# The order in which a head's query tiles have their row maxima sought, in self attention

## The chip, the cores and the metric

The kernel is one decoder layer in float32, written by hand in Bass with explicit semaphores. It runs on one core of a Trainium2 chip. The metric is the device time of one execution in microseconds (us), as the median of several executions.

## What is computed

The layer has three parts. Batch 4, sequence 1024, width 512, 16 heads of 32.

```python
x = _layernorm(tgt, n1_g, n1_b)
tgt = tgt + _block_sparse_self_attn(x, ...)     # causal, and keys/queries masked by a router
x = _layernorm(tgt, n2_g, n2_b)
tgt = tgt + _mha_cross(x, memory, ...)
x = _layernorm(tgt, n3_g, n3_b)
ff = jax.nn.relu(x @ ff_w1.T + ff_b1) @ ff_w2.T + ff_b2
return tgt + ff
```

The self attention is what the change touches:

```python
scores = jnp.einsum('bhqd,bhkd->bhqk', q, kh) / jnp.sqrt(jnp.float32(D))
...
causal = jnp.triu(jnp.ones((S, S), bool), k=1)
scores = jnp.where(causal[None, None], -jnp.inf, scores)
p = jax.nn.softmax(scores, axis=-1)
out = jnp.einsum('bhqk,bhkd->bhqd', p, vh)
```

## The kernel before

Both attentions come from one builder, `attention`; its tag is `b_` for the self attention (causal) and `e_` for the cross attention. A **group** is 4 heads of one batch entry; there are 16 groups, n = 0 to 15. While group n's softmax and output are computed, the row maxima of group n+1 are sought, because the softmax subtracts each query's maximum and the maxima have to be known before the scores proper are computed.

A **unit** is one query tile (128 queries) of one head: 8 tiles by 4 heads are 32 units. For unit u the tensor engine multiplies the tile's queries with the keys up to its diagonal (`max_scores`, L1200, tile name `b_nat`): tile t has (t+1) x 128 keys, so tile 0 has 128 and tile 7 has 1024. Up to 512 keys fill one PSUM bank, more of them two. VectorE then adds the causal mask and takes the row maximum in one custom instruction plus a short one that reads its accumulator (`maximum`, L1107) into one column of `b_neg_max`. Four PSUM banks serve this, counted 0 to 3. `bank_of` says which bank a unit begins in, and `reach` says how many units back the last user of those banks stands: with reach 2 the matmuls of unit u wait until the maximum of unit u-2 is done, with reach 3 until that of unit u-3 is.

```python
bank_of = [(0, 1, 2, 3, 0, 2, 0, 2)[u % KT] for u in range(UNITS)]
reach = [(2, 3, 3, 4, 3, 2, 2, 2)[u % KT] for u in range(UNITS)]
def unit_before(n, u):
    ...
    return n * UNITS + u + 1 - reach[u]
```

When all 32 maxima of a group are there, `turn_max` (L1206) transposes `b_neg_max` on the tensor engine into bank `TURN_BANK`; this is **the turn**. VectorE splits the result into a high and a low part (`split_max`, L1117 and L1119), and two DMAs put them as extra rows into the queries `b_qs` of the next group, for which that group's first scores wait.

The main work of a group are 12 **steps** k of 4 heads j: scores (L1217), exponential on ScalarE (L1029), additions on GpSimd (L1054), the product with the values (`weigh`, L1229, after head 2 of the next step), and twice per group a product with ones that sums the probabilities (`sum_up`, L1241; 24 records for query half 1 in step 3, 8 for half 0 in step 7). VectorE takes these sums through two transposes and a reciprocal (`invert`, L1128 to L1132) and copies the outputs out of PSUM (`copy_outs`, L1095). All engines work through their queues strictly in the order written.

Where each unit stands between the scores is set by `slot_of`: the planner gives each place (step k, head 0 or 1) some free time, and deals the units out in proportion to `unit_size`, their estimated time. Places are counted from TURN_HEAD in step 9, so that a group's maxima begin right behind the turn of the group before. In the last piece of the projection stage ahead (tile names `p_`), all 32 units of group 0 are done in eight batches of four, one batch behind each item of 12 matmuls (`leading`); the turn and the first units of group 1 (`early_units`) follow.

Of the kernel before, what the change touches and what calls it, by code (L numbers as in the profile page):

```python
# [7 lines left out]
ALU = mybir.AluOpType  # L8
ACT = mybir.ActivationFunctionType
AX = mybir.AxisListType  # L10
# [4 lines left out]
P = 128  # L15
B, S, D = 4, 1024, 512
# [11 lines left out]
KT = S // P  # L28
# [782 lines left out]
def attention(place, tag, sem, ident, q_hi, q_lo, k_hi, k_lo, v, out, vacated, keep=None, mask_qk=None,  # L811
# [6 lines left out]
    causal = keep is not None  # L818
    MAX_ROW = AUG + 1 if causal else AUG
    ROWS = MAX_ROW + 2  # L820


    steps = [(h, t, max(0, t * P - h * TOK) if causal else 0) for h in range(HALVES)
             for t in range((h + 1) * TOK // P if causal else KT)]
    last_step = {h: max(n for n, st in enumerate(steps) if st[0] == h) for h in range(HALVES)}
    NS, NBLOCKS = len(steps), len(steps) * HG
    UNITS = HG * KT
    TURN, TURN_HEAD, PE_TURN_HEAD, TURN_BANK = NS - 3, 2, 2 if causal else 3, 2

# [44 lines left out]
    for at in range(NBLOCKS):  # L876
        k, j = divmod((START + at) % NBLOCKS, HG)
        step_us = 0.3 + 3.1 * (TOK - steps[k][2]) / TOK
        free.append(max(0.1, step_us - busy[k]) / 2 if j in (0, 1) else 0)
    slot_of, acc = [], 0.0  # L880
    unit_size = [0.15 + 0.133 * ((u % KT) + 1 if causal else KT) for u in range(UNITS)]
    for u in range(UNITS):
        x, at = acc / sum(unit_size) * sum(free), 0
        while x >= free[at]:
# [13 lines left out]
        assert len(slot_of) == UNITS  # L898

    if causal:  # L900
        bank_of = [(0, 1, 2, 3, 0, 2, 0, 2)[u % KT] for u in range(UNITS)]
        reach = [(2, 3, 3, 4, 3, 2, 2, 2)[u % KT] for u in range(UNITS)]
    else:
        bank_of, reach = [u % 2 * 2 for u in range(UNITS)], [2] * UNITS

    def unit_bank(n, u):
        return 0 if narrow and n == 0 else bank_of[u]
# [20 lines left out]
    neg_max = place(tag + "neg_max", SMALL_AT + 256, [P, UNITS])  # L928
# [159 lines left out]
    def vector(dve):  # L1088
# [6 lines left out]
            dve.tensor_copy(outs[:, h, :], pv_ps).then_inc(outs_copied, 1)  # L1095

        def maximum(n, u):
            keys = ((u % KT) + 1) * P if causal else S
            banks = 2 if keys > 512 else 1
            dve.wait_ge(nat_ready, n * UNITS + u + 1)  # L1100
            if u == 0 and n >= 1:
                dve.wait_ge(max_turned, n)
            found = nat(unit_bank(n, u), banks)[:, :, 0:keys // banks]
            if causal:

                masked = mask_qk[:, S - keys:S].rearrange("p (b t) -> p b t", b=banks)
                dve.tensor_tensor_reduce(out=found, in0=found, in1=masked, scale=-1.0, scalar=3.0e38, op0=ALU.add,  # L1107
                                         op1=ALU.min, accum_out=neg_max[:, u:u + 1]).then_inc(maxed, 1)
            else:
                dve.tensor_reduce(neg_max[:, u:u + 1], found, AX.XY, ALU.max, negate=True).then_inc(maxed, 1)  # L1110

        def split_max(n):
            dve.wait_ge(max_turned, n + 1)
# [58 lines left out]
    def tensor(pe):  # L1172
# [8 lines left out]

        def max_scores(n, u):
            p = n % SETS
            j, t = divmod(u, KT)
            keys = (t + 1) * P if causal else S
            banks = 2 if keys > 512 else 1
            width = keys // banks
            rows = AUG + 1 if causal else AUG
            if u == 0:
                kept = KEPT if causal and p == 2 else 0  # L1190
                pe.wait_ge(loaded[p], ((n // SETS + 1) * LOADS + kept) * 16)
                if not causal and n < SETS:
                    pe.wait_ge(rows_set, n + 1)
            if bank_of[u] == TURN_BANK and u <= TURN_BANK and n >= 1:
                pe.wait_ge(max_split, n * 2)
            if unit_before(n, u) > 0:
                pe.wait_ge(maxed, unit_before(n, u))
            for bank in range(banks):
                cols = max(width, 256)
                last = pe.matmul(nat(unit_bank(n, u) + bank, 1)[:, 0, 0:cols], qs[p][0:rows, j, t * P:(t + 1) * P],  # L1200
                                 ks[p][0:rows, j, bank * width:bank * width + cols], start=True, stop=True)
            last.then_inc(nat_ready, 1)
# [860 lines left out]
```

## Time and profile before

| | us |
|---|---|
| median of 3 runs | 3193.87 |
| lowest and highest | 3188.46, 3200.21 |
| the profiled execution | 3189.28 |
| span of its trace | 3187.6 |

The trace covers the span from the first to the last instruction of the program, and the execution takes 1.7 us more than the span. The tensor engine (PE) is busy for most of it. In the views, PE is the matmuls, PEld the loads of their stationary operand, DVE is VectorE, ACT ScalarE, POOL GpSimd, and L followed by a number is the line of the kernel. A time in brackets is how long the engine stood idle ahead of the row, with what ended it. A tensor engine that waits for a semaphore shows as such an idle time; the matmuls behind it in its queue wait too.

### The profile page before, as it was taken

To read this page: it belongs to the slowest core of one execution; us is meant where nothing else is said; L and a number is where in the kernel's file an instruction comes from. 1 tells how busy PE (TensorE), PEld (TensorE's weight loads), DVE (VectorE), ACT (ScalarE), POOL (GpSimd) and SP (SyncE) were. 2 spreads that over 40 slices of the span, in tenths; PEclk is the share of its full clock that TensorE was granted. 3 is DMA by queue.
4 is the path that set the end of the run, shared out by engine and by line. 5 is a ranking of instruction groups with operands and counts; after the bars stand their busy time and mean duration, and the time that the engine had idled before them with its cause. 6 is when DMAs were issued, how large, how long until landed. Compare 5 with 4: busy or idle time off the path is not lost.

```text
span 3187.6 us, 39475 instructions
## 1 busy us (share of the span) xinstructions
PE 2980.7 (94%) x15242; PEld 1966.3 (62%) x15242; DVE 1758.3 (55%) x2864; ACT 1243.5 (39%) x2335; POOL 1907.5 (60%) x991
## 2 busy tenths in 40 slices
PE   7999999999999959789999999999879999999999
PEld 6888886444444427664444444444348888888887
DVE  4455656777777535666777777777742222222221
ACT  2212222555555533325666666666532111111111
POOL 3324333888888775437888888888768343333432
PEclk8999999999999979999999999999989999999999
DMA  6555774445455135734234242332122101011000
GB/s 208 176 165 186 227 220 127 107 108 111 108 117 116 41 119 184 212 133 105 63 72 89 54 104 57 79 82 58 54 67 89 40 27 40 14 40 33 34 14 14
DMA packets 199538, 310.17 MB, mean 97 GB/s; under 512 B 15011, under 2 KB 93363, under 8 KB 199347
## 3 DMA queue, kind: packets, MB, share of 16 engines
q1 hardware_dynamic: 199350, 307.64, 35.3%
q8 instruction: 121, 1.98, 0.3%
q14 instruction: 67, 0.55, 0.1%
HBM read 189.04 MB, written 117.44 MB: 96 GB/s over the span
## 4 chain that ended last, share of the span: by engine, by line
PE 53%; DVE 5%; DMA 2%; POOL 1%; issue 1%; ACT 1%; SPq 1%; DVEq 0%; POOLq 0%; ACTq 0%
PE m_ring L89 13%; PE m_o_ps L89 10%; PE e_st L1217 8%; PE e_pv L1229 7%; PE e_nat L1200 7%; PE c_ring L89 5%; PE e_st L1241 2%; DVE e_neg_max L1110 2%; DMA e_qs<-e_max_lo 1%; DMA c_x<-in_x 1%; DVE m_xt_lo L1577 1%; DMA c_w_raw<-in_ca_in_w 0%; DVE m_xt_hi L1575 0%; DVE m_ow_lo L1595 0%; DVE m_xn L1570 0%
## 5 line engine op out<-in xcount | busy, mean ns | idle before, releaser
L1054 POOL TENSOR_TENSOR e_probs<-e_probs 128x2048 f32<-128x2048 f32 x160 | 732.7, 4585 | 146.5 <-ACT e_probs L1029 141.7
L1029 ACT ACTIVATE e_probs<-e_st 128x512 f32<-128x512 f32 x1024 | 558.1, 598 | 361.5 <-PE e_st L1217 344.0
L1110 DVE TENSOR_REDUCE e_neg_max<-e_nat 128x1 f32<-128x1024 f32 x512 | 603.0, 1217 | 141.6 <-PE e_nat L1200 136.7
L1029 ACT ACTIVATE b_probs<-b_st 128x512 f32<-128x512 f32 (+3 forms) x768 | 340.4, 491 | 278.6 <-PE b_st L1217 269.5
L1107 DVE CUSTOM_DVE_ANT_0 b_nat<-b_nat,mask_qk 128x128 f32<-128x128 f32 (+7 forms) x512 | 374.4, 784 | 80.8 <-PE b_nat L1200 79.6
L1217 PE MATMUL e_st<-e_qs,e_ks 98*128 98x512 f32 x1024 | 396.3, 431 | 22.6 <-DVE e_turned_sums L1128 12.3
L1545 POOL TENSOR_TENSOR m_hid_lo<-m_hid,m_hid_hi 128x512 fp32r<-128x512 f32 x128 | 168.3, 1315 | 386.5 <-DVE m_hid_hi L1583 386.5
L1054 POOL TENSOR_TENSOR b_probs<-b_probs 128x1536 f32<-128x1536 f32 (+3 forms) x128 | 374.7, 2927 | 38.0 <-PE b_pv L1229 35.1
L1583 DVE CAST m_hid_hi<-m_hid 128x512 fp32r<-128x512 f32 x128 | 60.4, 472 | 575.4 <-ACT m_hid L1459 575.4
L1200 PE MATMUL e_nat<-e_ks,e_qs 96*128 96x512 f32 x1024 | 327.5, 401 | 26.2 <-DVE e_neg_max L1110 26.2
L1217 PEld LDWEIGHTS e_st<-e_qs,e_ks 98*128 98x128 f32 x1024 | 176.2, 189 | 275.9 <-ACT e_probs L1029 188.7
L1459 ACT ACTIVATE m_hid<-m_ring,m_b 128x512 f32<-128x512 f32 x128 | 88.1, 688 | 602.8 <-PE m_o_ps L89 553.2
L1229 PE MATMUL e_pv<-e_probs,e_vs 128*32 128x512 f32 x2048 | 276.3, 612 | 2.3 <-DVE e_outs L1095 1.6
L405 POOL TENSOR_TENSOR p_part_lo<-p_full,p_part_hi 128x512 fp32r<-128x512 f32 x96 | 125.0, 1306 | 223.6 <-ACT p_part_hi L379 223.5
L1217 PE MATMUL b_st<-b_qs,b_ks 99*128 99x512 f32 (+2 forms) x768 | 254.9, 384 | 3.6 <-ACT b_probs L1029 1.8
L1200 PEld LDWEIGHTS e_nat<-e_ks,e_qs 96*128 96x128 f32 x1024 | 190.6, 190 | 85.0 <-DVE e_neg_max L1110 43.1
L1200 PE MATMUL b_nat<-b_ks,b_qs 97*128 97x384 f32 (+4 forms) x768 | 207.9, 357 | 31.6 <-DVE b_neg_max L1107 30.4
L1217 PEld LDWEIGHTS b_st<-b_qs,b_ks 99*128 99x128 f32 x768 | 132.0, 189 | 152.1 <-ACT b_probs L1029 89.0
L89 PE MATMUL m_o_ps<-m_w_hi,m_hid_hi 128*128 128x512 f32 x512 | 202.0, 395 | 10.8 <-issue 5.5
L89 PE MATMUL m_ring<-m_xt_hi,m_w_hi 128*128 128x512 f32 x512 | 201.1, 393 | 3.2 <-issue 3.0
L89 PE MATMUL m_ring<-m_xt_lo,m_w_hi 128*128 128x512 f32 x512 | 200.6, 392 | 0.0
L89 PE MATMUL m_o_ps<-m_w_lo,m_hid_hi 128*128 128x512 f32 x512 | 200.5, 392 | 0.0
(182 smaller groups left out, 5164.0 us busy)
## 6 DMA issues: line engine op xcount, KB each, us to landing
b_qs<-sq_hi SPq DMA_DIRECT2D x32, 512.0 KB, 6.7
b_ks<-sk_hi SPq DMA_DIRECT2D x32, 512.0 KB, 11.1
e_qs<-cq_hi SPq DMA_DIRECT2D x32, 512.0 KB, 6.8
e_ks<-ck_hi SPq DMA_DIRECT2D x32, 512.0 KB, 13.4
ck_hi<-p_part_hi SPq DMA_DIRECT2D x32, 256.0 KB, 3.3
ck_lo<-p_part_lo SPq DMA_DIRECT2D x32, 256.0 KB, 3.7
cv<-p_tok_out SPq DMA_DIRECT2D x32, 256.0 KB, 3.0
p_x<-in_x SPq DMA_DIRECT2D x8, 1024.0 KB, 7.4
```

The lines of the kernel that those rows point to most:

```text
L89: last = pe.matmul(out, w, x, start=(start and n == 0 and m == 0), stop=(stop and n == len(pairs) - 1 and m == 2))
L405: pool.tensor_tensor(self.part_lo[:, n % self.PARTS, :], self.full[:, n % self.PARTS, :], self.part_hi[:, n % self.PARTS, :].bitcast(F32), ...
L1029: act.activation(probs[:, home(n, k), j, first:TOK], st_ps[:, bank_at("scores", blk), first:TOK], ACT.Exp).then_inc(exped, 1)
L1054: pool.tensor_tensor(into, into, probs[:, home(n, k), :, first:TOK], ALU.add).then_inc(added, 1)
L1107: dve.tensor_tensor_reduce(out=found, in0=found, in1=masked, scale=-1.0, scalar=3.0e38, op0=ALU.add, op1=ALU.min, accum_out=neg_max[:, u:u ...
L1110: dve.tensor_reduce(neg_max[:, u:u + 1], found, AX.XY, ALU.max, negate=True).then_inc(maxed, 1)
L1200: last = pe.matmul(nat(unit_bank(n, u) + bank, 1)[:, 0, 0:cols], qs[p][0:rows, j, t * P:(t + 1) * P], ks[p][0:rows, j, bank * width:bank * ...
L1217: pe.matmul(st_ps[:, bank, lo:TOK], ks[p][0:ROWS, j, t * P:(t + 1) * P], qs[p][0:ROWS, j, h * TOK + lo:(h + 1) * TOK], start=True, stop=Tr ...
L1229: last = pe.matmul(pv_ps[j * DH:(j + 1) * DH, first:TOK], vs[n % SETS][:, t, j * DH:(j + 1) * DH], probs[:, home(n, k), j, first:TOK], sta ...
L1241: last = pe.matmul(st_ps[j * DH:(j + 1) * DH, bank, :], ones[:], probs[:, home(n, k), j, :], start=(k == firsts_of[h][0]), stop=(k == firs ...
L1459: act.activation(hid[:, c % HIDS, :], bank_at("hidden", n), ACT.Relu, bias=b1_sb[:, c:c + 1]).then_inc(relu_done, 1)
L1545: pool.tensor_tensor(hid_lo[:, c % HIDS, :], hid[:, c % HIDS, :], hid_hi[:, c % HIDS, :].bitcast(F32), ALU.subtract).then_inc(hid_lo_done, 1)
```

## The change

The tiles of a head are taken in the order 2, 7, 5, 3, 1, 6, 4, 0 instead of 0 to 7. The banks and the reach of each position are written anew, the turn goes into bank 0, and the planner deals out the units by their new sizes. The column of `b_neg_max` stays that of the tile. The cross attention keeps its order, banks and places.

```diff
+    TILE_ORDER = (2, 7, 5, 3, 1, 6, 4, 0) if causal else tuple(range(KT))
+
+    def unit_tile(u):
+        return u // KT, TILE_ORDER[u % KT]
+
+    def unit_keys(u):
+        return (unit_tile(u)[1] + 1) * P if causal else S
+
+    def unit_column(u):
+        return u // KT * KT + unit_tile(u)[1]
...
-    TURN, TURN_HEAD, PE_TURN_HEAD, TURN_BANK = NS - 3, 2, 2 if causal else 3, 2
+    TURN, TURN_HEAD, PE_TURN_HEAD, TURN_BANK = NS - 3, 2, 2 if causal else 3, 0 if causal else 2
...
-    unit_size = [0.15 + 0.133 * ((u % KT) + 1 if causal else KT) for u in range(UNITS)]
+    unit_size = [0.15 + 0.133 * unit_keys(u) / P for u in range(UNITS)]
...
-        bank_of = [(0, 1, 2, 3, 0, 2, 0, 2)[u % KT] for u in range(UNITS)]
-        reach = [(2, 3, 3, 4, 3, 2, 2, 2)[u % KT] for u in range(UNITS)]
+        bank_of = [(1, 2, 0, 2, 3, 0, 2, 0)[u % KT] for u in range(UNITS)]
+        reach = [(3, 3, 2, 2, 3, 3, 2, 2)[u % KT] for u in range(UNITS)]
...
+    TURN_UNIT = min(u for u in range(UNITS) if TURN_BANK - bank_of[u] in range(2 if unit_keys(u) > 512 else 1))
...
-            if bank_of[u] == TURN_BANK and u <= TURN_BANK and n >= 1:
+            if u == TURN_UNIT and n >= 1:
                 pe.wait_ge(max_split, n * 2)
```

By `reach`, the matmuls of a tile wait in the new order as follows: tile 5 for the maximum of tile 2, tile 3 for that of tile 7, tile 4 for that of tile 1, tile 0 for that of tile 6 (reach 2); tile 2 for tile 6, tile 7 for tile 4, tile 1 for tile 7 and tile 6 for tile 5 (reach 3), where the first two reach back into the head before.

**The first place.** On the tensor engine, from the last scores of the next group's step 0 on (L1217 before, L1230 now; `b_nat` is the units' matmul with 128, 256, 384, 512 columns for tiles 0 to 3 and 2 x 320 to 2 x 512 for tiles 4 to 7, and at least 256 columns; the digit behind `b_nat` is the pair of banks, 0 for banks 0 and 1). Before:

```order
L1217 MATMUL b_st<-b_qs0_90,b_ks0_93 128x512
L1217 MATMUL b_st<-b_qs0_90,b_ks0_93 128x384
L1200 MATMUL b_nat1<-b_ks1_94,b_qs1_91 128x384 x2
L1200 MATMUL b_nat0<-b_ks1_94,b_qs1_91 128x448 x2
L1217 MATMUL b_st<-b_qs0_90,b_ks0_93 128x384
L1200 MATMUL b_nat1<-b_ks1_94,b_qs1_91 128x512 x2
L1217 MATMUL b_st<-b_qs0_90,b_ks0_93 128x384
L1229 MATMUL b_pv<-b_probs_99,b_vs2_98 32x128 x4
```

Now:

```order
L1230 MATMUL b_st<-b_qs0_90,b_ks0_93 128x512
L1230 MATMUL b_st<-b_qs0_90,b_ks0_93 128x384
L1213 MATMUL b_nat1<-b_ks1_94,b_qs1_91 128x512
L1213 MATMUL b_nat1<-b_ks1_94,b_qs1_91 128x256
L1213 MATMUL b_nat0<-b_ks1_94,b_qs1_91 128x448 x2
L1230 MATMUL b_st<-b_qs0_90,b_ks0_93 128x384
L1213 MATMUL b_nat1<-b_ks1_94,b_qs1_91 128x320 x2
L1213 MATMUL b_nat0<-b_ks1_94,b_qs1_91 128x256
L1230 MATMUL b_st<-b_qs0_90,b_ks0_93 128x384
L1242 MATMUL b_pv<-b_probs_99,b_vs2_98 32x128 x4
```

In steps 0 stand tiles 3, 1 and 6, then 4 and 0, where tiles 5 and 6, then 7 stood: five units instead of three.

**The second place.** The tensor engine from the sum of half 0 (L1241, now L1254) to the turn (L1206, now L1219). Before:

```order
L1241 MATMUL b_st<-b_probs_99,b_ones_105 32x512 x4
L1217 MATMUL b_st<-b_qs0_90,b_ks0_93 128x512
L1217 MATMUL b_st<-b_qs0_90,b_ks0_93 128x384
L1200 MATMUL b_nat1<-b_ks1_94,b_qs1_91 128x384 x2
L1217 MATMUL b_st<-b_qs0_90,b_ks0_93 128x384
L1200 MATMUL b_nat0<-b_ks1_94,b_qs1_91 128x448 x2
...
L1217 MATMUL b_st<-b_qs0_90,b_ks0_93 128x256
L1200 MATMUL b_nat1<-b_ks1_94,b_qs1_91 128x512 x2
L1217 MATMUL b_st<-b_qs0_90,b_ks0_93 128x256 x2
L1206 MATMUL b_nat1<-ident,b_neg_max_102 32x128
```

Now:

```order
L1254 MATMUL b_st<-b_probs_99,b_ones_105 32x512 x4
...
L1213 MATMUL b_nat1<-b_ks1_94,b_qs1_91 128x512
L1230 MATMUL b_st<-b_qs0_90,b_ks0_93 128x384
L1213 MATMUL b_nat1<-b_ks1_94,b_qs1_91 128x256
L1213 MATMUL b_nat0<-b_ks1_94,b_qs1_91 128x448 x2
...
L1213 MATMUL b_nat1<-b_ks1_94,b_qs1_91 128x320 x2
L1230 MATMUL b_st<-b_qs0_90,b_ks0_93 128x256
L1213 MATMUL b_nat0<-b_ks1_94,b_qs1_91 128x256
L1230 MATMUL b_st<-b_qs0_90,b_ks0_93 128x256
L1219 MATMUL b_nat0<-ident,b_neg_max_102 32x128
```

Between the sum and the turn stand tiles 3, 1, 6, 4 and 0 where tiles 5, 6 and 7 stood; the last one is tile 0, one matmul ahead of the turn.

**The third place.** On VectorE, between the reciprocal of half 0 and the split (each maximum is two rows, of which the second, the accumulator's read, is left out here). Before:

```order
L1132 STREAM_TRANSPOSE b_turned_sums<-b_inverse 128x512
L1107 ISA b_nat,b_neg_max<-b_nat,mask_qk 128x2x384
...
L1107 ISA b_nat,b_neg_max<-b_nat,mask_qk 128x2x448
...
L1107 ISA b_nat,b_neg_max<-b_nat,mask_qk 128x1024
...
L1117 CAST b_max_hi<-b_nat 32x128
```

Now:

```order
L1145 STREAM_TRANSPOSE b_turned_sums<-b_inverse 128x512
L1120 ISA b_nat,b_neg_max<-b_nat,mask_qk 128x512
...
L1120 ISA b_nat,b_neg_max<-b_nat,mask_qk 128x256
...
L1120 ISA b_nat,b_neg_max<-b_nat,mask_qk 128x2x448
...
L1120 ISA b_nat,b_neg_max<-b_nat,mask_qk 128x2x320
...
L1120 ISA b_nat,b_neg_max<-b_nat,mask_qk 128x128
```

Five maxima of 2432 keys in all take the place of three of 2688 keys. In the projection stage the batches of four units are now tiles 2, 7, 5, 3 and tiles 1, 6, 4, 0, where they were tiles 0 to 3 and 4 to 7.

## Rows read from the trace of the kernel before

**Rows 1.** Busy time by engine in one group of self attention.

```profile
core 0: us, PE busy (x) PEld busy (x) DVE busy (x) ACT busy (x) POOL busy (x), PEclk, DMA share, GB/s
795.87:833.92 38.05, 35.24 (x227) 18.28 (x225) 28.81 (x74) 21.39 (x49) 30.54 (x19) 1.00 0.52 112
```

**Rows 2.** Waits of 524 to 1095 us: total, times, longest.

```profile
PE b_nat L1200 <- DVE b_neg_max L1107: 25.7, 74, 0.7
PE b_nat L1206 <- DVE b_neg_max L1107: 15.1, 15, 1.0
```

**Rows 3.** Timeline of PE in that group: start, us.

```profile
796.05 0.93 PE L1200 MATMUL b_nat<-b_ks,b_qs 97*128 97x384 f32 x4
796.81 0.34 PE L1217 MATMUL b_st<-b_qs,b_ks 99*128 99x384 f32 x1
797.67 0.73 PE L1200 MATMUL b_nat<-b_ks,b_qs 97*128 97x512 f32 x2 [0.52 <-DVE b_neg_max L1107]
798.25 0.33 PE L1217 MATMUL b_st<-b_qs,b_ks 99*128 99x384 f32 x1
...
821.84 1.04 PE L1241 MATMUL b_st<-b_probs,b_ones 128*32 128x512 f32 x8
...
826.06 0.63 PE L1200 MATMUL b_nat<-b_ks,b_qs 97*128 97x512 f32 x2
826.53 0.54 PE L1217 MATMUL b_st<-b_qs,b_ks 99*128 99x256 f32 x2
828.08 0.28 PE L1206 MATMUL b_nat<-ident,b_neg_max 128*32 128x128 f32 x1 [1.01 <-DVE b_neg_max L1107]
```

**Rows 4.** Timeline of DVE in that group.

```profile
796.60 0.97 DVE L1107 CUSTOM_DVE_ANT_0 b_nat<-b_nat,mask_qk 128x768 f32<-128x768 f32 x1 [1.10 <-PE b_nat L1200]
...
797.48 1.13 DVE L1107 CUSTOM_DVE_ANT_0 b_nat<-b_nat,mask_qk 128x896 f32<-128x896 f32 x1
...
798.53 1.27 DVE L1107 CUSTOM_DVE_ANT_0 b_nat<-b_nat,mask_qk 128x1024 f32<-128x1024 f32 x1
...
799.71 0.69 DVE L1095 COPY b_outs<-b_pv 128x512 f32<-128x512 f32 x1
...
811.95 0.29 DVE L1107 CUSTOM_DVE_ANT_0 b_nat<-b_nat,mask_qk 128x128 f32<-128x128 f32 x1
...
812.16 0.46 DVE L1107 CUSTOM_DVE_ANT_0 b_nat<-b_nat,mask_qk 128x256 f32<-128x256 f32 x1
...
812.54 0.60 DVE L1107 CUSTOM_DVE_ANT_0 b_nat<-b_nat,mask_qk 128x384 f32<-128x384 f32 x1
...
813.06 0.73 DVE L1107 CUSTOM_DVE_ANT_0 b_nat<-b_nat,mask_qk 128x512 f32<-128x512 f32 x1
...
813.70 0.86 DVE L1107 CUSTOM_DVE_ANT_0 b_nat<-b_nat,mask_qk 128x640 f32<-128x640 f32 x1
814.49 0.14 DVE L1107 DVE_READ_ACCUMULATOR2_ANT b_neg_max<- 128x1 f32 x1
...
824.62 0.93 DVE L1107 CUSTOM_DVE_ANT_0 b_nat<-b_nat,mask_qk 128x768 f32<-128x768 f32 x1
...
827.88 0.14 DVE L1107 DVE_READ_ACCUMULATOR2_ANT b_neg_max<- 128x1 f32 x1
```

**Rows 5.** Waits of 483 to 524 us, the projection stage's end.

```profile
PE b_nat L1200 <- DVE b_neg_max L1107: 4.7, 8, 0.9
```

**Rows 6.** Timeline there, PE and DVE, one head of four.

```profile
483.76 0.81 PE L1200 MATMUL b_nat<-b_ks,b_qs 97*128 97x256 f32 x4
484.41 0.40 PE L89 MATMUL p_ring<-p_x_hi,p_w_hi 128*128 128x512 f32 x1
...
487.15 0.81 PE L1200 MATMUL b_nat<-b_ks,b_qs 97*128 97x320 f32 x4
...
487.96 0.82 DVE L1107 CUSTOM_DVE_ANT_0 b_nat<-b_nat,mask_qk 128x640 f32<-128x640 f32 x1
...
490.38 0.40 PE L89 MATMUL p_ring<-p_x_hi,p_w_hi 128*128 128x512 f32 x1
```

More of the change, by code:

```diff
@@ L1097, in maximum @@
         def maximum(n, u):
-            keys = ((u % KT) + 1) * P if causal else S
+            keys = unit_keys(u)
             banks = 2 if keys > 512 else 1
@@ L1107, in maximum @@
                 dve.tensor_tensor_reduce(out=found, in0=found, in1=masked, scale=-1.0, scalar=3.0e38, op0=ALU.add,
-                                         op1=ALU.min, accum_out=neg_max[:, u:u + 1]).then_inc(maxed, 1)
+                                         op1=ALU.min, accum_out=neg_max[:, unit_column(u):unit_column(u) + 1]).then_inc(maxed, 1)
             else:
-                dve.tensor_reduce(neg_max[:, u:u + 1], found, AX.XY, ALU.max, negate=True).then_inc(maxed, 1)
+                dve.tensor_reduce(neg_max[:, unit_column(u):unit_column(u) + 1], found, AX.XY, ALU.max, negate=True).then_inc(maxed, 1)
         def split_max(n):
@@ L1183, in max_scores @@
             p = n % SETS
-            j, t = divmod(u, KT)
-            keys = (t + 1) * P if causal else S
+            j, t = unit_tile(u)
+            keys = unit_keys(u)
             banks = 2 if keys > 512 else 1
```

## The prediction

> **What bounds the kernel now.** The change touches only the self attention and the end of the projection stage ahead of it, so I read only those stretches. First the busy time of one group [rows 1]: in 38.05 us the tensor engine (PE) is busy for 35.24, VectorE (DVE) for 28.81. PE is the bound, but not all of its time is work. Next the waits [rows 2]: over the stage PE stands idle for 25.7 us ahead of the units' matmuls (L1200) and for 15.1 us ahead of 15 turns (L1206), both times for DVE's maxima. Per group (15 groups seek maxima) that is 1.7 and 1.0 us, which is nearly all of the 38.05 - 35.24 = 2.8 us that PE is idle. So what the change can win is here and nowhere else, and every wait it adds in PE's queue costs its full length: scores, values and sums stand behind it.
>
> The idle time is less than the delay. In step 0 tile 7's matmul should follow the scores of 796.81 by 0.23 us, at 797.04; it starts at 797.67, 0.63 late, of which the row calls 0.52 idle; and it then takes 0.58 to the next scores where an unblocked tile 7 takes 0.47 (826.06 to 826.53) [rows 3]. I put a blocked unit at its idle time and 0.25 us (0.2 by this row; a one-bank unit is shorter and hides more of its wait). Six units per group are blocked: 1.7 + 6 x 0.25 = 3.2 us. The turn comes 1.55 us behind the scores at 826.53, where 0.4 would do: 1.15 us.
>
> **Durations of the parts.** From one start to the next on DVE [rows 4] a maximum takes: tile 0 0.21, tile 1 0.38, tile 2 0.52, tile 3 0.64, tile 4 0.79, tile 5 0.88, tile 6 1.05, tile 7 1.18 us. A PE instruction that waits for it starts 0.20 after that (827.88 to the turn at 828.08 [rows 3, 4]). DVE starts 0.55 after the first of tile 5's matmuls (796.05 to 796.60); for one-bank units I take 0.4. On PE tiles 5 and 6 together cost 0.76 (796.05 to 796.81), tile 7 0.47, tiles 0 to 3 together 0.65 (483.76 to 484.41 [rows 6]); by columns that is 0.12, 0.12, 0.17, 0.24 for tiles 0 to 3 and 0.30, 0.35, 0.41 for tiles 4 to 6.
>
> **What the change does not touch.** The same 32 units per group, the same instructions, bytes and banks in use. The sum of PE's work is equal, DVE's too. Only waits can differ. The turn's bank differs, but the unit that waits for the split (tile 5, in step 11) comes some 4 us behind it; cost 0.
>
> **The step where units are densest: step 0.** From the group's first scores at 0, PE issues tile 3 at 0.18, tile 1 at 0.42, tile 6 at 0.54, scores at 0.95, and would issue tile 4 at 1.17. Tile 4 waits for tile 1's maximum: DVE starts tile 3 at 0.6, tile 1 at 1.27, is done at 1.65, PE goes on at 1.85: a wait of 0.68, and 0.10 for the slower restart. Tile 0 would follow at 2.25 and waits for tile 6's maximum, 1.65 + 1.05 + 0.20 = 2.90: 0.65 + 0.10. Together 1.53 us, where before tile 7's wait was 0.73.
>
> **The other steps,** walked in the same way, with the queue of DVE as written: steps 1 to 4 lose their wait (before, tile 2 waited for tile 7 in step 1; now nothing is due before its bank is free). In step 5 tile 7 is 0.24 late (tile 4's maximum stands behind the reciprocal of half 1) and tile 5 is 0.63 late behind tile 2, which stands behind the copy of the outputs. In step 6 tile 4 waits for tile 1 again: 0.76. In step 7 tile 5 waits for tile 2: 0.35. Sum up to the sum of half 0: 1.53 + 0.24 + 0.63 + 0.76 + 0.35 = 3.5 us, against 3.2 before: **+0.3 us** per group. I can't read these from a row of before, since the neighbours are new; an error of 0.1 at each of five places is 0.5 per group.
>
> **From the sum of half 0 to the turn** the chain is DVE's, before and now. Before: sum issued 821.84, reciprocal done and first maximum started 824.62, three maxima back to back to 827.88, turn 828.08: 2.78 + 3.26 + 0.20 = 6.24 us [rows 3, 4]. Now: 2.78, then tiles 3, 1, 6, 4, 0: 0.64 + 0.38 + 1.05 + 0.79 + 0.21 = 3.07, and 0.20: 6.05. So **-0.2 us** per group. That the last one is small doesn't free the turn: tile 0's own matmul waits for tile 6's maximum (its bank), and tile 4's maximum stands between. Of the turn's wait of 1.15 some 0.6 moves up to tile 0's matmul and 0.6 stays. From the turn to the next group's first scores (row DMAs) nothing changes.
>
> Per group +0.3 - 0.2 = +0.1 us; 15 groups: **+1.5 us**.
>
> **The eight batches in the projection stage.** Here four units stand together with nothing between them. Before, tiles 0 to 3 have no wait (0.65 in all), tiles 4 to 7 take 487.15 to 490.38 = 3.23 where their matmuls need 1.53: 1.70 lost per head [rows 6], of which the view of waits calls 4.7 us in 8 waits idle [rows 5]. Now, in the first batch, with DVE starting 0.81 after the batch's first matmul (487.15 to 487.96, its drain of the projection comes first): tile 2 done 1.33, tile 5 may start 1.53 (due 0.64); tile 7 done 1.33 + 1.18 = 2.51, tile 3 may start 2.70 (due 1.98); batch ends 3.04 where 1.23 would do: 1.81 lost. Second batch: tile 1 done 1.19, tile 4 starts 1.39 (due 0.53); tile 6 done 2.24, tile 0 starts 2.44 (due 1.79); batch ends 2.66 where 0.95 would do: 1.71 lost. 3.52 - 1.70 = 1.82 per head, 4 heads: **+7.3 us**. PE is never idle there but for these waits, so nothing hides them.
>
> **Sum.** +1.5 + 7.3 = +8.8 us on the profiled execution's 3189.28 us, 3198.1. That execution lies 4.6 below the median of 3193.87, so against the median I say 3202.7, rounded 3203: +0.28%.
>
> **A rule on the restart.** The 0.10 us is the difference of two rows, 0.58 and 0.47 [rows 3]. The Trainium skill (TensorE: Matmul & The Clock Gate, Step-by-step: what each phase is for) says that matmuls stay in program order and that only weight loads are pulled ahead of them. The first half is what makes each wait cost all that is queued behind. By the second half a blocked unit's weights would be there when it is released and the 0.10 would be nothing; the trace speaks against it here. By that the sum per group would be 0.1 smaller (seven blocked units now, six before), 1.5 us in all.
>
> **Rivals.**
> *Only places change (3189 on the profile, 3194 on the median).* Four banks and one DVE queue serve the same 32 units, and what is lost in the batches is won back elsewhere: tiles 5 or 3 could be let go earlier than I walk. For it: the sum per group is a difference of two like numbers, 3.5 and 3.2, so 0.5 per group less is enough to cancel the 7.3. Against it: the batches have no play. Chance 0.20. The Trainium skill (Perfetto Trace Analysis, Optimization Strategy) has a rule that points here: a gap that repeats through a stretch can mean that PSUM is short for the next tile; the number of banks is the same before and now. The repeating gaps of the trace agree with it.
> *Faster: the alternation hides the waits.* If small and large tiles really balance, those waits of steps 0, 5, 6 and 7 vanish in which tiles 4 and 5 wait for the small tiles 1 and 2: 0.78 + 0.63 + 0.76 + 0.35 = 2.5, so 3.5 falls to 1.0. Against 3.2 that is -2.2, with the turn's -0.2 it is -2.4 per group, -36 in 15 groups, and +7.3: 3161 on the profile, 3165 on the median. For it: in steps 1 to 4 the walk finds no waits. Against it: DVE would have to reach tile 1's maximum 0.7 us earlier than the 1.27 above, but it can't begin tile 3 before its matmul. It decides from 0.7 us of lead on DVE. It need only come half as far to count as faster. Chance 0.12.
> *Slower: DVE falls behind in steps 5 to 7.* There the reciprocal, a copy and seven maxima stand close. If the reciprocal of half 1 ends 0.5 us later than I walk, the blocked units of steps 5 and 6 (three) each start 0.5 later, 1.5 per group, and the sum, and with it the DVE chain to the turn, is late by the same: 15 x 1.5 = 22, with 8.8 it is 31: 3220 on the profile, 3225 on the median. For it: each of these units has less than 0.2 us of play. Against it: a later PE gives DVE time, so only the first wait should count in full. It decides from 0.3 us per group. Chance 0.20.
>
> **How the numbers follow.** The forecast above has 0.48. Its own range is 3196 to 3211: 0.5 us per group for the walk, either way. A difference below 0.5% (16 us) can't be told from none here, so forecast and first rival both say same: 0.68; faster 0.12, slower 0.20. The range for 8 in 10 goes from 3186 (the first rival, and some of the second) to 3222 (most of the way to the third).
>
> **What the profile after should show.** The stage's wait at the turn falls from 1.0 to about 0.4 us idle each; the waits ahead of units' matmuls rise from 25.7 to about 28 to 34 us; the waits of the batches rise from 4.7 to about 9 us in 16 waits; from the sum of half 0 to the turn 6.05 us; a group of 38.0 to 38.4 us; PE's busy time and the clock as before. The prediction is wrong if the waits up to the sum are far from 3.5 us per group, or if the batches lose no more than before.

## The result, and the profile after

| | before | after |
|---|---|---|
| median, us (15 runs each) | 3193.87 | 3207.59 |
| lowest and highest | 3187.17, 3200.21 | 3199.70, 3237.45 |
| the profiled execution | 3189.28 | 3211.38 |
| span of its trace | 3187.6 | 3209.7 |

The ratio is 1.0047, with a 95% interval of 1.0035 to 1.006: slower by 0.47%, just below the bound of 0.5%, with an interval that reaches past it. The forecast was 3203 in a range of 3186 to 3222. The two profiled executions differ by 22.1 us, more than the medians (13.7). Of the 22.1, 4.3 us lie ahead of the first unit (483.76 before [rows 6], 488.02 now), where nothing is changed; from there to the start of group 15, the last one and the only one that seeks no maxima, it is 16.1 us, and behind that 1.7.

The page of the profile after, its busy times and the line of the granted clock in 40 slices:

```profile
PE 3001.6 (94%) x15242; PEld 1976.9 (62%) x15242; DVE 1761.3 (55%) x2864; ACT 1244.5 (39%) x2335; POOL 1906.8 (59%) x991
PEclk9899999999999978999999999999989999999999
```

The number of matmuls is that of before, yet the tensor engine is busy for 20.9 us more (2980.7 before). The same matmuls took longer, so the clock must be looked at. First the waits, of the stage as in [rows 2] and then of the batches as in [rows 5]:

```profile
PE b_nat L1213 <- DVE b_neg_max L1120: 29.8, 63, 0.7
PE b_nat L1219 <- DVE b_neg_max L1120: 7.8, 14, 0.6
```

```profile
PE b_nat L1213 <- DVE b_neg_max L1120: 7.1, 12, 0.7
```

The windows cut the two kernels at different places: the last head's two batches lie behind 524 us here, so that 2.4 of the 29.8 us are theirs. Counted by what they belong to, the batches' waits went from 4.7 in 8 to 9.5 in 16 (forecast about 9 in 16) and the groups' from 25.7 to 27.4 (forecast 28 to 34). At the turn 0.56 us are left of 1.0 (forecast 0.4). Busy time and clock by stretch: an ordinary group, a longer one, 3.4 us inside the longer one, and 3.4 us behind a batch:

```profile
core 0: us, PE busy (x) PEld busy (x) DVE busy (x) ACT busy (x) POOL busy (x), PEclk, DMA share, GB/s
851.76:889.71 37.95, 35.35 (x226) 18.36 (x225) 29.00 (x74) 21.44 (x49) 30.53 (x19) 1.00 0.51 112
927.73:967.26 39.53, 36.92 (x227) 18.97 (x226) 29.12 (x74) 21.43 (x48) 30.56 (x19) 0.96 0.49 108
932.20:935.60 3.40, 3.40 (x14) 1.42 (x13) 1.87 (x5) 1.08 (x4) 2.10 (x3) 0.50 0.87 207
502.10:505.50 3.40, 3.40 (x10) 2.63 (x9) 1.17 (x4) 0.00 (x0) 0.00 (x0) 0.50 0.23 86
```

The same view of the kernel before, over its groups:

```profile
524.00:1100.00 576.00, 532.34 (x3373) 278.43 (x3371) 432.26 (x1111) 321.44 (x723) 450.99 (x266) 1.00 0.49 106
```

The ordinary group takes 37.95 us, 0.1 less than before [rows 1], with full clock. The longer one takes 1.6 more, all of it busy time of PE, and has 3.4 us in which the granted clock is 0.50, the lower of the two levels, 1.2 instead of 2.4 GHz. There are seven such stretches of 3.4 us in the changed part: behind two batches (502.1 and 526.0) and in five groups (549.9, 587.4, 778.6, 932.2, 1085.8). Before had none up to 1104.6 us. That is in group 15, 4 us behind its start, where each trace of this study has one of 7 to 10 us; it isn't the change's.

Step 0 of the ordinary group on PE (the scores at 852.70 and 854.84, tile 4 and tile 0 between them), and, in a view of its own, the load of tile 0's stationary operand:

```profile
852.70 0.34 PE L1230 MATMUL b_st<-b_qs,b_ks 99*128 99x384 f32 x1
853.57 0.56 PE L1213 MATMUL b_nat<-b_ks,b_qs 97*128 97x320 f32 x2 [0.52 <-DVE b_neg_max L1120]
854.61 0.39 PE L1213 MATMUL b_nat<-b_ks,b_qs 97*128 97x256 f32 x1 [0.49 <-DVE b_neg_max L1120]
854.84 0.34 PE L1230 MATMUL b_st<-b_qs,b_ks 99*128 99x384 f32 x1
```

```profile
854.61 0.19 PEld L1213 LDWEIGHTS b_nat<-b_ks,b_qs 97*128 97x128 f32 x1 [0.75 <-DVE b_neg_max L1120]
```

Counted from the group's first scores, 851.76, the two units start at 1.81 and 2.85 and the next scores at 3.08; the prediction had 1.85, 2.90 and 3.12. Two idle times of half a microsecond stand 1 us apart. In the longer group, the same place and what follows it:

```profile
929.48 0.56 PE L1213 MATMUL b_nat<-b_ks,b_qs 97*128 97x320 f32 x2 [0.52 <-DVE b_neg_max L1120]
930.52 0.39 PE L1213 MATMUL b_nat<-b_ks,b_qs 97*128 97x256 f32 x1 [0.49 <-DVE b_neg_max L1120]
...
931.78 1.02 PE L1213 MATMUL b_nat<-b_ks,b_qs 97*128 97x384 f32 x3
932.60 0.63 PE L1230 MATMUL b_st<-b_qs,b_ks 99*128 99x256 f32 x2
933.15 1.08 PE L1242 MATMUL b_pv<-b_probs,b_vs 128*32 128x512 f32 x4
```

The waits are the same to 0.01 us; then, from 932.2 on, the matmuls take twice as long: four matmuls of the values take 1.08 us at 933.15, where four of the same shape take 0.61 to 0.64 elsewhere. So the waits alone don't say in which group the clock falls, but each of the five falls begins 3 to 5 us into a group, behind these two waits. Nor does it look like chance alone: the last three falls, at 778.6, 932.2 and 1085.8, are 153.6 us apart each time, which is every fourth group.

One batch of the projection stage, the second head's tiles 2, 7, 5 and 3:

```profile
499.10 0.81 PE L1213 MATMUL b_nat<-b_ks,b_qs 97*128 97x384 f32 x3
500.58 0.62 PE L1213 MATMUL b_nat<-b_ks,b_qs 97*128 97x384 f32 x2 [0.67 <-DVE b_neg_max L1120]
501.76 0.52 PE L1213 MATMUL b_nat<-b_ks,b_qs 97*128 97x512 f32 x1 [0.56 <-DVE b_neg_max L1120]
502.10 0.61 PE L89 MATMUL p_ring<-p_x_hi,p_w_hi 128*128 128x512 f32 x1
```

Two waits 1.2 us apart here as well. But a batch of the old order has such a pair too, tiles 6 and 7 of the kernel before, 0.92 us apart; it has one per head where the new order has two:

```profile
488.89 0.68 PE L1200 MATMUL b_nat<-b_ks,b_qs 97*128 97x448 f32 x2 [0.93 <-DVE b_neg_max L1107]
489.81 0.73 PE L1200 MATMUL b_nat<-b_ks,b_qs 97*128 97x512 f32 x2 [0.24 <-DVE b_neg_max L1107]
```

The last row of the batch after, at 502.10, is the first matmul of the next item, at half clock: 0.61 us where the same matmul takes 0.40 in [rows 6]. And from the sum to the turn of the ordinary group, PE, then VectorE's rows for tiles 6 and 4:

```profile
877.79 1.04 PE L1254 MATMUL b_st<-b_probs,b_ones 128*32 128x512 f32 x8
...
882.15 0.46 PE L1213 MATMUL b_nat<-b_ks,b_qs 97*128 97x320 f32 x2
882.45 0.28 PE L1230 MATMUL b_st<-b_qs,b_ks 99*128 99x256 f32 x1
...
883.84 0.28 PE L1219 MATMUL b_nat<-ident,b_neg_max 128*32 128x128 f32 x1 [0.56 <-DVE b_neg_max L1120]
```

```profile
881.54 1.12 DVE L1120 CUSTOM_DVE_ANT_0 b_nat<-b_nat,mask_qk 128x896 f32<-128x896 f32 x1
882.58 0.14 DVE L1120 DVE_READ_ACCUMULATOR2_ANT b_neg_max<- 128x1 f32 x1
882.65 0.83 DVE L1120 CUSTOM_DVE_ANT_0 b_nat<-b_nat,mask_qk 128x640 f32<-128x640 f32 x1
```

From sum to turn it is 6.05 us, as forecast. Tile 0's matmul (882.77) has no idle time of PE ahead of it, where the prediction let some 0.6 us of the turn's wait move up to it. VectorE is through with tile 6 at 882.6, and PE's matmuls of tile 4, which its maximum needs, are issued at 882.15 to 882.30: tile 4's maximum could hardly begin earlier by either.

### The profile page after: what moved, and what is told of

The parts are those of the page before. It is cut to its first block, busy times and chain, and to the rows that moved or that the text cites. A ratio compares the mean times of both kernels' runs of the same rounds, so it can differ in the third digit from the quotient of the medians.

```text
span 3209.7 us, 39475 instructions
## 1 busy us (share of the span) xinstructions
PE 3001.6 (94%) x15242; PEld 1976.9 (62%) x15242; DVE 1761.3 (55%) x2864; ACT 1244.5 (39%) x2335; POOL 1906.8 (59%) x991
## 4 chain that ended last, share of the span: by engine, by line
PE 52%; DVE 5%; DMA 2%; POOL 1%; issue 1%; ACT 1%; SPq 1%; DVEq 0%; POOLq 0%; ACTq 0%
PE m_ring L89 13%; PE m_o_ps L89 10%; PE e_st L1230 8%; PE e_pv L1242 7%; PE e_nat L1213 7%; PE c_ring L89 5%; PE e_st L1254 2%; DVE e_neg_max L1123 2%; DMA e_qs<-e_max_lo 1%; DMA c_x<-in_x 1%; DVE m_xt_lo L1590 1%; DMA c_w_raw<-in_ca_in_w 0%; DVE m_xt_hi L1588 0%; DVE m_ow_lo L1608 0%; DVE m_xn L1583 0%
## 5 line engine op out<-in xcount | busy, mean ns | idle before, releaser
L1120 DVE CUSTOM_DVE_ANT_0 b_nat<-b_nat,mask_qk 128x384 f32<-128x384 f32 (+7 forms) x512 | 374.9, 782 | 87.5 <-PE b_nat L1213 87.0
L1230 PE MATMUL e_st<-e_qs,e_ks 98*128 98x512 f32 x1024 | 397.6, 432 | 21.9 <-DVE e_turned_sums L1141 12.3
L1230 PEld LDWEIGHTS e_st<-e_qs,e_ks 98*128 98x128 f32 x1024 | 176.6, 190 | 276.0 <-ACT e_probs L1042 188.9
L1230 PE MATMUL b_st<-b_qs,b_ks 99*128 99x512 f32 (+2 forms) x768 | 258.4, 389 | 3.7 <-ACT b_probs L1042 1.7
L1213 PE MATMUL b_nat<-b_ks,b_qs 97*128 97x384 f32 (+4 forms) x768 | 209.2, 361 | 39.1 <-DVE b_neg_max L1120 36.9
L1230 PEld LDWEIGHTS b_st<-b_qs,b_ks 99*128 99x128 f32 x768 | 133.6, 193 | 157.6 <-ACT b_probs L1042 82.8
L89 PE MATMUL m_o_ps<-m_w_hi,m_hid_lo 128*128 128x512 f32 x512 | 200.2, 391 | 0.0
```

What stands on the lines that cost most here:

```text
L89: last = pe.matmul(out, w, x, start=(start and n == 0 and m == 0), stop=(stop and n == len(pairs) - 1 and m == 2))
L1230: pe.matmul(st_ps[:, bank, lo:TOK], ks[p][0:ROWS, j, t * P:(t + 1) * P], qs[p][0:ROWS, j, h * TOK + lo:(h + 1) * TOK], start=True, stop=Tr ...
```

## The experiments

Two theories of the loss. **Waits**: it is the 7 us that the batches wait longer, and nothing else. **Waits and clock**: to these come the stretches at half clock, and what brings them is the two waits that stand close together (tile 4 and tile 0 in step 0; in a batch tiles 5 and 3, 4 and 0). For each kernel the trace gives the time from the first unit to group 0's step 0 (the batches), and from there to group 15's (the groups). The differences to before (48.6 and 567.9 us) are set against the ratio in one table; 0.001 is 3.2 us. The times are those of one trace each, the ratios those of the medians of 5 to 15 runs.

| kernel | batches | groups | half clock behind batches, in groups 0 to 14 | ratio, interval |
|---|---|---|---|---|
| after | +10.1 | +6.0 | 2, 5 | 1.0047, 1.0035 to 1.0060 |
| again | +10.2 | +6.1 | 2, 5 | 1.0058, 1.0041 to 1.0075 |
| lead_old | 0.0 | +4.7 | 0, 4 | 1.0021, 1.0009 to 1.0032 |
| lead_new | +10.2 | 0.0 | 2, 0 | 1.0025, 1.0014 to 1.0035 |
| t0_later | +10.1 | -4.5 | 2, 0 | 1.0018, 1.0005 to 1.0030 |
| two_waits | +1.6 | +11.3 | 1, 6 | 1.0028, 1.0013 to 1.0043 |
| rotate | +2.7 | +16.8 | 1, 1 | 1.0056, 1.0044 to 1.0068 |
| best | +1.6 | -3.2 | 1, 0 | 0.9988, 0.9979 to 0.9998 |
| best_split | +1.6 | -3.5 | 1, 0 | 0.9986, 0.9977 to 0.9994 |
| early | +1.5 | +4.4 | 1, 2 of 6.8 us | 1.0016, 1.0004 to 1.0029 |
| early_split | +1.5 | -3.0 | 1, 1 | 0.9994, 0.9985 to 1.0003 |

**The change once more** (again), as a measure of what repeats.

> The changed kernel as it is, a second time. In its first trace the TensorE clock was granted at half speed for 3.4 us seven times in the changed stretch (twice behind a batch of the projection stage, five times behind step 0 of a group), which never happened there before; each cost 1.5 to 1.7 us. If the two close waits of a batch or of step 0 bring that on, such stretches stand in this trace too, behind the same places though not in the same groups, 4 to 10 of them, and the time is 3207 within 5. If they were chance, there are none or they stand anywhere, and the time may be nearer 3200.

1.0058, and half clock at the same kinds of places: 501.5 and 525.4 behind batches, 549.3, 586.8, 740.4, 931.6 and 1085.2 in groups. The number repeats, the groups that are hit only in part. In lead_old and two_waits below, most falls in the groups are again evenly spaced: 153.6 us apart in lead_old (groups 2, 6, 10 and 14) and 116.05 us apart in two_waits (groups 3, 6, 9 and 12; groups 0 and 14 are out of step).

**The two halves of the change** (lead_old, lead_new). The batches of group 0 get an order, banks and reach of their own. lead_old has the old ones there and the new ones in the groups, lead_new the new ones there and the old ones in the groups.

```diff
+    LEAD_ORDER = (0, 1, 2, 3, 4, 5, 6, 7) if causal else tuple(range(KT))
...
-    def unit_tile(u):
-        return u // KT, TILE_ORDER[u % KT]
+    def unit_tile(u, n=1):
+        return u // KT, (TILE_ORDER if n else LEAD_ORDER)[u % KT]
```

> Group 0's units in the projection stage go back to tiles 0 to 7 and their old banks; all other groups keep the new order. By my theory (batches lose 1.7 us more per head, and two half-speed stretches) it is 7 + 3 = 10 us faster than the changed kernel: about 3197, ratio to before 1.001, with 8 waits of 4.7 us idle in the batches. If the batches' loss is hidden by something behind them, it stays at 3207.

> The reverse: only group 0's units in the projection stage take the new order and banks; the groups 1 to 15 have the old one. By my theory 7 us for the batches and up to 3 for half-speed stretches behind them: 3194 + 7 to 10 = 3201 to 3204, ratio 1.002 to 1.003, and no half-speed stretch in the groups. If the order in the groups is what costs the time, it is 3194.

1.0021 (1.001 was expected) and 1.0025, together 1.0046: within their intervals of 0.001 either way the halves add up to the whole, and each is near half of it. For the batches 10.2 us are too many for the waits alone: they are 6.9 us of waits (1.73 per head) and 3.2 at half clock. In the groups nothing but the clock is left: the ordinary group of lead_old takes 37.95 us, 0.1 less than before, and four take about 39.5; 4 x 1.5 - 15 x 0.09 = 4.7, the table's number.

```profile
836.85:874.80 37.95, 35.37 (x227) 18.39 (x225) 29.02 (x74) 21.45 (x49) 30.50 (x19) 1.00 0.51 112
912.77:952.23 39.46, 36.89 (x227) 18.91 (x226) 29.07 (x74) 21.43 (x49) 30.52 (x19) 0.96 0.49 109
```

**One of the two waits away** (t0_later): the new order, but tile 0 of the first head (unit 7) goes from step 0, head 1 to step 1, head 0 (slot 4), away from tile 4.

```diff
+        slot_of[7] = 4
```

> The changed kernel with one unit moved: tile 0 of the first head goes from step 0, place 1 to step 1, place 0, so that it no longer waits for tile 6's maximum (step 0 keeps one wait of 0.5 us instead of two). By the walk alone 0.75 us in 15 groups: 11 us faster than the changed kernel, 3196. If two waits close together also bring the half-speed clock, these stretches vanish from the groups too, some 7 us more: 3189. If the wait only moves on to tile 7 or to the turn, it stays at 3207.

The groups win 4.5 us on before and 10.6 on the change, and none of them has half clock. Step 0 in it, then the product with the values in step 1, then the group as a whole:

```profile
849.30 0.56 PE L1226 MATMUL b_nat<-b_ks,b_qs 97*128 97x320 f32 x2 [0.52 <-DVE b_neg_max L1133]
849.70 0.33 PE L1243 MATMUL b_st<-b_qs,b_ks 99*128 99x384 f32 x1
...
852.43 0.64 PE L1255 MATMUL b_pv<-b_probs,b_vs 128*32 128x512 f32 x4 [0.33 <-ACT b_probs L1055]
```

```profile
847.50:885.31 37.81, 35.36 (x226) 18.36 (x225) 28.82 (x74) 21.47 (x49) 30.55 (x19) 1.00 0.51 112
```

Counted from the group's start the scores behind tile 4 come at 2.20 in place of 3.08: 0.9 us gained at the place. 0.12 of that is tile 0's own matmul, which has only moved. At the end of the group 0.14 is left (37.81 against 37.95): a new wait of 0.33 us for ScalarE's exponentials takes the old one's place in step 1, and PE's other idle times in the group are those of the change to 0.02 us. The expectation had 0.75 us per group, 11 in all, for the waits alone. So 15 x 0.14 = 2 us of the 10.6 are waits, and five stretches at half clock that are gone are 7.5 more, at 1.5 each; 1 us is left over.

**The two waits in the old order** (two_waits): the kernel before, with tile 0 of the second head (unit 8) moved from step 1, head 0 to step 0, head 1 (slot 1), right behind tile 7.

```diff
+        slot_of[8] = 1
```

> The kernel before with one unit moved: tile 0 of the second head goes from step 1, place 0 to step 0, place 1, right behind tile 7, where it has to wait for tile 6's maximum. Step 0 then holds two close waits of some 0.5 us idle each, in the old order. If that is what halves the clock, 3.4 us stretches at half speed appear behind step 0 in three to six of the groups, each group of 38.0 us being 1.5 us longer, and none in the batches: 6 us and up to 3 us of waiting, 3197 to 3203. If the new order itself or anything else in the changed kernel brings the stretches on, there are none and it is 3194 to 3197.

Step 0 of an ordinary group of it, an ordinary and a longer group, and the stretch within:

```profile
847.34 0.73 PE L1226 MATMUL b_nat<-b_ks,b_qs 97*128 97x512 f32 x2 [0.53 <-DVE b_neg_max L1133]
848.39 0.39 PE L1226 MATMUL b_nat<-b_ks,b_qs 97*128 97x256 f32 x1 [0.32 <-DVE b_neg_max L1133]
```

```profile
845.53:883.72 38.19, 35.30 (x226) 18.27 (x225) 28.80 (x74) 21.23 (x49) 30.51 (x19) 1.00 0.50 111
883.72:923.35 39.63, 36.76 (x226) 18.73 (x225) 28.79 (x74) 21.43 (x49) 30.49 (x19) 0.96 0.49 108
888.00:891.40 3.40, 3.40 (x14) 1.30 (x14) 2.07 (x7) 1.45 (x4) 2.21 (x3) 0.50 0.82 186
```

Six groups have half clock, in a trace that is otherwise that of before, and the 11.3 us of the table are 6 x 1.5 for them and 15 x 0.16 for the new wait (38.20 against 38.04). The order of the tiles isn't needed for it; two idle times, 0.5 and 0.3 us, 1.05 us apart, do it. (One batch has half clock too, which wasn't expected.) The sum of both experiments is what shows the cause in the groups: taken out of the new order they take the half clock away, put into the old one they bring it.

**A third order** (rotate): tiles 1 to 7 and then 0, with the old batches. Like the change it ends on the smallest tile, but the large ones stay together.

```diff
+    TILE_ORDER = (1, 2, 3, 4, 5, 6, 7, 0) if causal else tuple(range(KT))
...
+        bank_of = [(1, 2, 3, 0, 2, 0, 2, 0)[u % KT] for u in range(UNITS)]
+        reach = [(3, 3, 4, 3, 2, 2, 2, 2)[u % KT] for u in range(UNITS)]
```

> Smallest last without alternation: tiles 1 to 7, then 0; group 0 in the projection stage in the old order. The planner puts tiles 6, 7 and 0 behind the reciprocal. If the turn is set by VectorE's queue, it comes 2.78 + 1.05 + 1.18 + 0.21 + 0.20 = 5.4 us after the sum of half 0 was issued (6.24 before, 6.05 in the changed kernel), with 0.3 us idle ahead of it. If the last unit's size is what counts, the interval is that of the changed kernel, which also ends with tile 0, 6.0 us. No two close waits in step 0, so no half-speed stretches. Step 7 gets denser; in all 3185 to 3195.

This one went against both expectations: each group takes 39.1 us, with full clock but for one stretch, and the turn comes 6.5 us behind the sum, later than in either kernel. The rows of VectorE ahead of the turn show why (the sum is at 875.85, the turn at 882.35):

```profile
878.64 1.09 DVE L1129 CUSTOM_DVE_ANT_0 b_nat<-b_nat,mask_qk 128x896 f32<-128x896 f32 x1
879.65 0.14 DVE L1129 DVE_READ_ACCUMULATOR2_ANT b_neg_max<- 128x1 f32 x1
880.76 1.23 DVE L1129 CUSTOM_DVE_ANT_0 b_nat<-b_nat,mask_qk 128x1024 f32<-128x1024 f32 x1 [0.97 <-PE b_nat L1222]
881.91 0.33 DVE L1129 CUSTOM_DVE_ANT_0 b_nat<-b_nat,mask_qk 128x128 f32<-128x128 f32 x1
```

VectorE stands idle for 0.97 us ahead of tile 7, whose matmuls the tensor engine has in step 9's first place, 4.24 us behind the sum. That isn't VectorE's queue: it is the place of the last large tile in PE's own program. Before, tile 7 stands at the same distance, 4.22 us [rows 3], and the turn follows at 6.24; here tile 0's maximum comes on top, 0.25. A smallest tile at the end buys nothing while the large one ahead of it keeps its place. The turn is only 0.26 us of the 1.1 that a group loses. Over the 15 groups the units' waits are 33.0 us in place of 25.7, those ahead of the turns 18.8 in place of 15.1, and 3.5 us of waiting for the transposed sums are new, 0.24 per group.

**Old batches and tile 0 later** (best): what the runs so far point to.

> lead_old and t0_later together: the old order in the batches, the new one in the groups, without the second wait of step 0. No half-speed stretch should be left in the changed stretch, and a group takes the 37.8 us seen in t0_later against 38.05 before: 5 us faster than before, 3188, ratio 0.998 to 0.999. If the gains don't add (stretches come back elsewhere), 3194 or more.

0.9988: faster than before by 3.8 us and than the change by 19. The first is less than the bound of 0.5%, though its interval ends just short of 1. The groups take 37.8 us as expected, but for one that has, at full clock, a wait of 1.75 us for the DMA of the split's rows (at 988.37). One stretch at half clock is left, behind a batch. Between lead_old and best lies the place of this one unit, and the medians go from 1.0021 to 0.9988 with it, by intervals that don't meet.

**What sets the turn** (best_split, early, early_split). In best_split the reciprocal of half 0 and the transpose behind it, 0.95 us of VectorE's work, move behind the split. In early the last two units, tiles 4 and 0 of the last head, come earlier on PE (slots 34 and 36): tile 4 in step 8 at head 2 instead of step 9, tile 0 in step 9 at head 0 instead of head 1. early_split has both.

```diff
             dve.transpose(turned_sums[:], st_ps[:, bank_at("sums", done), :]).then_inc(sums_turned, 1)
+            if not (causal and h == 0):
+                invert_rest(n, h)
...
                             split_max(n + 1)
+                        if causal and k == TURN and j == TURN_HEAD:
+                            invert_rest(n, 0)
...
+        slot_of[30] = 34
+        slot_of[31] = 36
```

> best, with the reciprocal and second transpose of half 0 (0.95 us of VectorE) moved from step 8 to behind the split of step 9; the first transpose stays. If VectorE's queue between sum and turn sets the turn, it comes 0.6 to 0.9 us earlier (some 5.2 us after the sum in place of 6.05), its 0.55 us of idle time goes, and 15 groups give 8 to 10 us: 3179, ratio 0.995 to 0.996. If the tensor engine's own work sets it, no change against best: 3188.

> The version with tile 0 moved to step 1 and the old order in the batches (0.9988 of the time before), with the last two units of a group, tile 4 and tile 0 of head 3, placed one place earlier: tile 4 at the end of step 8 and tile 0 in the first place of step 9. Theory two equal paths (from the sum to the turn VectorE's queue and the tensor engine's own placement of tile 4 take equally long): only one of the two is shortened, so the turn stays at 6.05 us behind the sum (5.9 to 6.1), and the time at 0.997 to 1.000. Rival, the tensor engine's placement alone sets the turn: 5.3 to 5.5 us, 0.6 less in 15 groups, 9 us, 0.994 to 0.997.

> The same, and the end of the reciprocal of half 0 (0.95 us of VectorE's work) behind the split as well, so that both paths are shortened. Theory two equal paths: the turn comes about 0.7 us earlier, 5.3 to 5.5 us behind the sum, a group takes 37.1 to 37.3 us in place of 37.8, 15 x 0.6 = 9 us less, 0.994 to 0.997. Rival, VectorE has slack already and something third sets the turn (the maximum of tile 6 behind its own matmul): 6.0 us, 0.998 to 1.000.

From the sum to the turn it is 6.05 us in best, 6.05 in best_split, 6.67 in early and 5.83 in early_split (904.55 to 911.22 and 867.40 to 873.23 in the last two). Of best_split, VectorE's tiles 6 and 4; then of early, PE's tile 4, the scores ahead of the turn, and the turn; then the last two rows of early_split:

```profile
865.79 1.13 DVE L1133 CUSTOM_DVE_ANT_0 b_nat<-b_nat,mask_qk 128x896 f32<-128x896 f32 x1
...
867.74 0.83 DVE L1133 CUSTOM_DVE_ANT_0 b_nat<-b_nat,mask_qk 128x640 f32<-128x640 f32 x1 [0.76 <-PE b_nat L1233]
```

```profile
908.49 0.56 PE L1228 MATMUL b_nat<-b_ks,b_qs 97*128 97x320 f32 x2 [0.91 <-DVE b_neg_max L1135]
...
910.99 0.38 PE L1245 MATMUL b_st<-b_qs,b_ks 99*128 99x256 f32 x1 [0.22 <-ACT b_probs L1057]
911.22 0.27 PE L1234 MATMUL b_nat<-ident,b_neg_max 128*32 128x128 f32 x1
```

```profile
873.01 0.38 PE L1252 MATMUL b_st<-b_qs,b_ks 99*128 99x256 f32 x1 [0.22 <-ACT b_probs L1057]
873.23 0.27 PE L1241 MATMUL b_nat<-ident,b_neg_max 128*32 128x128 f32 x1
```

With VectorE freed, it idles for 0.76 us until PE brings tile 4, and the turn stays where it was: a second path, PE's own placement, is as long. With PE's placement shortened alone, tile 4 waits 0.91 us for its bank, everything behind it waits too, and the turn comes 0.6 us later. Two of these groups have half clock for 6.8 us (from 985.0 and 1063.5), both right behind tile 4's wait; the one from 955.11 takes 40.51 us in place of 38.0:

```profile
985.00:991.80 6.80, 6.80 (x27) 2.88 (x27) 2.23 (x8) 1.86 (x6) 4.79 (x3) 0.50 0.02 6
```

In the 4 us ahead of these two falls that wait of 0.91 is the only one of more than 0.1 us, so here a single wait was enough, in 2 of 15 groups.

In early I had expected the turn where it was: that a unit placed too early costs what stands behind it is the one thing I left out. With both shortened the turn has no wait at all, but comes only 0.2 us earlier instead of 0.6 to 0.7: the scores ahead of it now wait 0.22 us for ScalarE, in each group. A third engine stands close behind the other two. And the 0.21 us are not kept: up to the sum a group of early_split takes 26.12 us where one of best takes 25.88, with a wait of 0.58 us for ScalarE in step 1 that was 0.32 there. The kernel stays at 0.9994, no better than best.

## Why the prediction was right, and what it left out

The prediction was right in its sign, in its range and in most of its steps: 3203 in 3186 to 3222, measured 3207.59. But in the stretch that the change touches it had 8.8 us where the traces have 16.1. The larger part of that, 11 us, has a cause that the prediction left out, and two small errors cancel some of it. That the number still fell into the range is owed to the width of the range, which was made for other rivals; so far it is luck.

- **The batches** lost 1.73 us per head where 1.82 were forecast, 6.9 for 7.3 in all. The walk by durations held, unit by unit: in the second head, counted from its first matmul at 499.10, tile 5 starts at 1.48 and tile 3 at 2.66 (forecast 1.53 and 2.70).
- **Step 0** held to 0.05 us: 1.81, 2.85 and 3.08 where 1.85, 2.90 and 3.12 were forecast.
- **Steps 5 to 7** wait less than forecast: tile 7 in step 5 not at all (0.24), tile 5 0.37 us idle, tile 4 in step 6 0.48, tile 5 in step 7 0.09. With 0.25 for each of these three they are as forecast to 0.03 us, and the way up to the sum loses about 3.2 us in place of 3.5. The 3.2 that it was compared with is too large in its turn: it takes six blocked units per group, but [rows 2] have 74 waits in 15 groups, five each, which makes 2.95. By the starts, group to sum takes 26.03 us now and 25.97 before: +0.06 in place of +0.3.
- **From the sum to the turn** 6.05 us, forecast 6.05. The number is right and its reason only half: the text says that the chain is VectorE's. best_split took 0.95 us out of that chain and the turn didn't move. Two chains of equal length end there. From the turn to the next group it is 5.87 us, 5.84 before.
- So an ordinary group is 0.1 us shorter than before, not 0.1 longer: -1.3 us (15 x 0.09) in place of +1.5.
- **"PE's busy time and the clock as before"** is the step that failed. The change brings seven stretches of 3.4 us at half clock, 1.5 to 1.6 us each, 11 in all. The sum of the prediction with the measured terms is 6.9 - 1.3 + 11 = 16.6 us against the 16.1 of the traces; the forecast of 8.8 was too small by the clock and too large by 3.2 us elsewhere. Of the 11 us, 7.8 are in the groups, where taking out one wait and putting one in show the cause. The 3.2 behind the batches are less sure to be the change's: before has none there, but six of the eight traces with the old batches have one stretch, against two in each of four traces with the new ones.
- **The rivals.** "Only places change" is out: the batches lose what was forecast. The gain of 36 us is out too: tile 4 waits in step 0 as walked. The slower rival named the right sign of the error and the wrong mechanism; VectorE doesn't fall behind in steps 5 to 7. The clock was no rival at all, though the prediction's own walk of step 0 has the two waits in it that bring it down.
- **The restart.** The prediction weighed 0.10 us for it against a rule of the Trainium skill by which it would be nothing. The rows speak for the 0.10: a blocked tile 0 takes 0.23 us to the next scores (854.61 to 854.84), an unblocked one 0.12 (865.84 to 865.96); an unblocked tile 4 takes 0.30 (882.15 to 882.45 in the trace after), a blocked one 0.40 (849.30 to 849.70 in t0_later). The rows of PEld fit this: the load of the blocked tile 0 starts with its matmul at 854.61, not ahead of it, while that of the unblocked tile 4 starts 0.11 us ahead of its matmul at 882.15:

```profile
882.04 0.31 PEld L1213 LDWEIGHTS b_nat<-b_ks,b_qs 97*128 97x128 f32 x2
```

In the kernel the wait stands in the queue ahead of both, load and matmul; that this is the reason is argued and not tested. The Trainium skill's rule (TensorE: Matmul & The Clock Gate, Step-by-step: what each phase is for) names the array's rows and the background buffer as what lets a load go ahead, and says nothing of a load behind a wait.

Open is what picks the groups that are hit. The same two waits, equal to 0.01 us, stand in each of 15 groups and bring half clock in four to six of them; the even spacing of most of the falls (153.6 and 116.05 us) says that the pick is in part regular, and no run here varies it. Open is also why a wait of 1.0 us at each turn of the kernel before, or of 1.25 in rotate, brings none where 0.91 in early did twice. rotate and early_split have one fall each in group 0, behind waits of 0.61 and 0.53 us with one of 0.23 near them. I have shown that the two waits bring the half clock in some groups and that it goes when one of them goes, not what exactly is asked of them, nor that it takes two.

## What to carry to other kernels

A walk through the queues with durations from the trace foretold the starts in step 0 and in the batches to 0.05 us and is worth its trouble, but it must ask of each new wait whether another stands close to it: here two waits of half a microsecond, 1 us apart, cost 1 us where they stand and in a third of the groups 1.5 more in the clock. Spreading them was worth it, even at the price of a third wait of 0.33 us. And before a stretch is called the chain of one engine, take some work out of it: at this turn VectorE's chain and PE's were equally long and ScalarE's scores stood some 0.2 us behind them, and each cure showed the next.

## What was not expected of the hardware

- Two idle times of 0.52 and 0.49 us, 1 us apart, on a tensor engine that is otherwise busy can be followed by 3.4 us at a granted clock of 0.50 (932.20 to 935.60); in early a single one of 0.91 us was followed by 6.8 us of it, twice. The Trainium skill has a case of this kind from another kernel (TensorE: Matmul & The Clock Gate, A second HAM failure mode: psum-queue depth-cycling): short and frequent idles between groups of matmuls, as PSUM banks are cycled, make the clock swing between its two levels. This case's trace agrees: 0.50 and 1.00 by stretch, with the banks' waits ahead.
- A unit that was blocked takes 0.10 to 0.11 us longer to what follows it than one that was not, with one matmul (0.23 for 0.12) as with two (0.40 for 0.30); its load starts only with the release.
